# Expert outputs of a four-layer model: ScalarE copies both banks, and products with a stacked identity add and turn them

## The reference

```python
h = tok(ids, adj, rel)                                 # embeddings and a neighbour sum
h = h + attn0(norm(h)); h = h + experts16(norm(h))     # 16 experts, 2 chosen, relu, then a norm
h = h + attn1(norm(h)); h = h + experts4(norm(h))      # 4 experts, routed by attention over a graph, gelu
h = h + attn2(norm(h)); h = h + experts8(norm(h))      # 8 experts, 2 chosen, gelu
h = h + attn3(norm(h)); h = h + experts8_gated(norm(h))# 8 experts, silu(x w1) * (x w3), then w2
# every expert part:
out = sum over e of gate[:, e] * (act(x @ w1[e] + b1[e]) @ w2[e] + b2[e])
```

## Time and profile before

| | |
|---|---|
| runs of the kernel before | 947.99, 953.34, 950.22 us; median 950.22 |
| the profiled execution | 948.82 us |
| its span, first to last instruction | 947.0 us |
| mean granted TensorE clock | 0.933 of full speed |
| TensorE busy | 828.5 us |
| VectorE busy | 642.7 us |
| ScalarE busy | 372.0 us |
| POOL busy | 231.4 us |

### The profile page before, as it was taken

One profiled execution on the slowest core, in us unless ns is written; L12 is line 12 of the kernel. 1 busy time (PEld: TensorE's weight loads), 2 busy tenths in 40 slices (PEclk: granted clock), 3 DMA queues, 4 the chain that ended last, 5 costly groups with the idle time before them and its releaser, 6 DMA issues. The chain is left out here.

```text
span 947.0 us, 18228 instructions
## 1 busy us (share of the span) xinstructions
PE 828.5 (87%) x7272; PEld 455.8 (48%) x7272; DVE 642.7 (68%) x1722; ACT 372.0 (39%) x644; POOL 231.4 (24%) x292
## 2 busy tenths in 40 slices
PE   0896879979997887998888879999999998987997
PEld 0466757755533335773366533333333444444543
DVE  3979558878885548997754776556566457557665
ACT  0222444344653343223542523545454333244433
POOL 1900003314535113440150041113132414110000
PEclk9898989988999999998975987999999999797999
DMA  9500030000000001000000000000000000000000
GB/s 295 136 1 2 1 94 2 2 2 2 1 1 2 0 2 48 1 2 1 1 1 1 2 1 1 1 1 2 1 1 2 1 2 1 2 1 1 7 7 12
DMA packets 11360, 15.16 MB, mean 16 GB/s; under 512 B 8262, under 2 KB 9318, under 8 KB 10278
## 3 DMA queue, kind: packets, MB, share of 16 engines
q1 hardware_dynamic: 9856, 12.89, 4.4%
q10 hardware_dynamic: 1418, 1.09, 0.5%
HBM read 13.45 MB, written 0.52 MB: 15 GB/s over the span
## 5 line engine op out<-in xcount | busy, mean ns | idle before, releaser
L996 DVE TENSOR_REDUCE mx<-PS 128x2 f32<-128x1024 f32 (+3 forms) x96 | 102.5, 1088 | 69.5 <-PE PS L772 57.8
L937 ACT ACTIVATE arena<-PS 128x1024 f32<-128x1024 f32 (+3 forms) x96 | 85.8, 917 | 126.4 <-PE PS L813 113.4
L804 PE MATMUL PS<-arena 32*128 32x512 f32 (+3 forms) x384 | 88.7, 609 | 6.7 <-ACT arena L923 2.7
L829 PE MATMUL PS<-arena 128*64 128x512 f32 (+3 forms) x384 | 93.5, 571 | 0.4 <-DVE arena L1055 0.4
L772 PE MATMUL PS<-arena 32*128 32x512 f32 (+3 forms) x384 | 89.7, 635 | 4.4 <-DVE arena L979 3.8
L1537 ACT ACTIVATE arena<-PS,f_b_sb 128x512 f32<-128x512 f32 x96 | 61.2, 684 | 42.0 <-PE PS L1468 38.9
L1563 DVE TENSOR_TENSOR arena<-arena,PS 128x512 f32<-128x512 f32 x96 | 61.6, 683 | 16.0 <-PE PS L1479 15.9
L1468 PE MATMUL PS<-XT,late 64*64 64x512 f32 x384 | 62.5, 621 | 2.7 <-issue 1.3
L1499 PE MATMUL PS<-arena,late 64*64 64x512 f32 x384 | 57.3, 595 | 0.9 <-DVE arena L1563 0.9
L1100 POOL TENSOR_TENSOR H<-H,arena 128x256 f32<-128x256 f32 x32 | 23.5, 735 | 120.1 <-DVE arena L1030 117.7
L804 PEld LDWEIGHTS PS<-arena 32*128 32x128 f32 x384 | 27.3, 189 | 51.3 <-issue 32.8
(11 more groups left out here) (481 smaller groups left out, 1761.0 us busy)
## 6 DMA issues: line engine op xcount, KB each, us to landing
arena<-in_rel SPq DMA_DIRECT2D x4, 1024.0 KB, 12.0
late<-in_edges SPq DMA_DIRECT2D x2, 1024.0 KB, 11.5
arena<-in_adj SPq DMA_DIRECT2D x1, 1024.0 KB, 6.9
late<-in_w_f_w SPq DMA_DIRECT2D x2, 512.0 KB, 3.9
Cc<-in_consts SPq DMA_DIRECT2D x1, 916.0 KB
arena<-in_ids ACTq DMA_DIRECT2D x1, 800.0 KB
late<-in_w_f_w SPq DMA_DIRECT2D x2, 340.0 KB, 3.7
late<-in_w_f_w SPq DMA_DIRECT2D x4, 128.0 KB, 2.8
```

What stands on the lines that cost most here:

```text
L804: ins = nc.tensor.matmul(PS[:, a + j, queries(g, c)], KT[h, g % 3, c * P:(c + 1) * P], QT[h, g % 3, queries(g, c)], start=not less_first, ...
L829: ins = nc.tensor.matmul(PS[half(j), 6 + p, queries(g, c)], XO[:, batch(g) * TB + c, :], PT[:, s % 2, p, j, queries(g, c)], start=c == 0, ...
L937: nc.scalar.activation(PT[:, s % 2, p, :, queries(g, c)], PS[:, a:a + 2, queries(g, c)], ACT.Exp, scale=of(g).scale).then_inc(exp_done.sem, 1)
L996: v.reduce_max(mx[:, g % 2, c, 2 * p:2 * p + 2], PS[:, a:a + 2, keys(g, c)], axis=AX.X).then_inc(max_done.sem, 1)
```

## The change

ScalarE now copies both banks, into `OT` and a new `OT2`, and counts `out_copied` up by two a batch. VectorE's sum is gone, with `out_summed`. The turn is no longer four transposes but eight f32 products with `C["twin"]` as the moving operand: for each of four chunks of 128 tokens one product has the chunk of `OT` as weights and one the chunk of `OT2`, both accumulated in the same 64 columns of PSUM. A product with `twin` turns the chunk and adds its two halves of partitions; the accumulation adds the two banks. So what comes out is the batch's output itself, 256 columns instead of 512, and VectorE adds it to the residual in one addition instead of two. `half_added` is gone. TensorE's wait before the next batch's first `down` and before the turn is now for both copies.

```diff
@@ shared
     OT = part(3584, [2, S])
+    OT2 = part(4608, [2, S])
-    out_summed = Signal(ctx, nc, "out_summed")
-    half_added = Signal(ctx, nc, "half_added")
@@ experts, TensorE
                         if b >= 1:
-                            eng.wait_ge(out_copied.sem, c0 + b)
+                            eng.wait_ge(out_copied.sem, c0 + 2 * b)
                         if b >= 2:
                             eng.wait_ge(out_added.sem, a0 + b - 1)
...
                 def turn(b):
-                    eng.wait_ge(out_summed.sem, s0 + b + 1)
+                    eng.wait_ge(out_copied.sem, c0 + 2 * b + 2)
                     for t in range(TB):
-                        ins = nc.tensor.transpose(PS[:, out_banks(b)[1], t * P:(t + 1) * P], OT[:, b % 2, t * P:(t + 1) * P], ident)
+                        for part_sums in (OT, OT2):
+                            ins = nc.tensor.matmul(PS[:, out_banks(b)[1], t * D:(t + 1) * D], part_sums[:, b % 2, t * P:(t + 1) * P], C["twin"], start=part_sums is OT, stop=part_sums is OT2, skip_group_check=True)
                     ins.then_inc(turned_done.sem, 1)
@@ experts, ScalarE
                         nc.scalar.copy(OT[:, b % 2, :], PS[:, out_banks(b)[0], :]).then_inc(out_copied.sem, 1)
+                        nc.scalar.copy(OT2[:, b % 2, :], PS[:, out_banks(b)[1], :]).then_inc(out_copied.sem, 1)
@@ experts, VectorE
-                        turned = PS[:, out_banks(b)[1], :].rearrange("p (t m d) -> p t m d", m=2, d=D)
+                        turned = PS[:, out_banks(b)[1], 0:TB * D].rearrange("p (t d) -> p t d", d=D)
                         eng.wait_ge(turned_done.sem, t0 + b + 1)
-                        v.tensor_tensor(dst[:, y, :], turned[:, :, 0], base[:, y, :], ALU.add).then_inc(half_added.sem, 1)
-                        eng.wait_ge(half_added.sem, f0 + b + 1)
-                        v.tensor_tensor(dst[:, y, :], turned[:, :, 1], dst[:, y, :], ALU.add).then_inc(out_added.sem, 1)
+                        v.tensor_tensor(dst[:, y, :], turned, base[:, y, :], ALU.add).then_inc(out_added.sem, 1)
...
-                    if ends(k - LAG):
-                        b = tiles[2 * (k - LAG)][0]
-                        eng.wait_ge(out_copied.sem, c0 + b + 1)
-                        v.tensor_tensor(OT[:, b % 2, :], PS[:, out_banks(b)[1], :], OT[:, b % 2, :], ALU.add).then_inc(out_summed.sem, 1)
```

More of the change, by code:

```diff
@@ L1433, in experts @@
         u0, g0, d0, t0 = up_done.count, gates_done.count, down_done.count, turned_done.count
-        h0, k0, c0, s0, f0, a0 = hidden_done.count, gated_done.count, out_copied.count, out_summed.count, half_added.count, out_added.count
+        h0, k0, c0, a0 = hidden_done.count, gated_done.count, out_copied.count, out_added.count
         RU, RG = 3, 2
@@ L1585, in _ @@
                 eng.wait_ge(out_added.sem, a0 + B)
-        for signal, n in ((up_done, U), (gates_done, U), (down_done, U), (turned_done, B), (hidden_done, U), (gated_done, U), (out_copied, B), (out_summed, B),
-                          (half_added, B), (out_added, B)):
+        for signal, n in ((up_done, U), (gates_done, U), (down_done, U), (turned_done, B), (hidden_done, U), (gated_done, U), (out_copied, 2 * B),
+                          (out_added, B)):
             signal.count += n
@@ L1608, in experts_by_gated_inputs @@
         u0, l0, g0, d0, t0 = up_done.count, linear_done.count, gates_done.count, down_done.count, turned_done.count
-        h0, x0, k0, c0, s0, f0, a0 = hidden_done.count, inputs_gated.count, gated_done.count, out_copied.count, out_summed.count, half_added.count, out_added.count
+        h0, x0, k0, c0, a0 = hidden_done.count, inputs_gated.count, gated_done.count, out_copied.count, out_added.count
         def pair(r):
@@ L1749, in _ @@
                             entered["last_gates_out"]()
[L1750 to L1753, removed]
                     if 2 <= j <= U + 1 and steps[j - 2][1] == SPB - 1:
@@ L1756, in _ @@
                         y = slice(b * TB, (b + 1) * TB)
-                        turned = PS[:, out_banks(b)[1], :].rearrange("p (t m d) -> p t m d", m=2, d=D)
+                        turned = PS[:, out_banks(b)[1], 0:TB * D].rearrange("p (t d) -> p t d", d=D)
                         eng.wait_ge(turned_done.sem, t0 + b + 1)
-                        nc.vector.tensor_tensor(dst[:, y, :], turned[:, :, 0], base[:, y, :], ALU.add).then_inc(half_added.sem, 1)
-                        eng.wait_ge(half_added.sem, f0 + b + 1)
-                        nc.vector.tensor_tensor(dst[:, y, :], turned[:, :, 1], dst[:, y, :], ALU.add).then_inc(out_added.sem, 1)
+                        nc.vector.tensor_tensor(dst[:, y, :], turned, base[:, y, :], ALU.add).then_inc(out_added.sem, 1)
                 eng.wait_ge(out_added.sem, a0 + B)
         for signal, k in ((up_done, U), (linear_done, U), (gates_done, 4 * B), (down_done, U), (turned_done, B), (hidden_done, 2 * U), (inputs_gated, 4 * B),
-                          (gated_done, 2 * U), (out_copied, B), (out_summed, B), (half_added, B), (out_added, B)):
+                          (gated_done, 2 * U), (out_copied, 2 * B), (out_added, B)):
             signal.count += k
```

## The result

The changed kernel takes 971.61 us, the median of four runs (970.15 to 975.41); the kernel before, beside it, 949.11 (four runs). The ratio is 1.0229, with a 95% interval of 1.0179 to 1.028. The forecast was 958.5 in a range of 952 to 967: slower, as said, but by 22.5 us instead of 8.3. The first rival's number, 971, is where it came out.

The account below looks back on a forecast made before the run. TensorE was taken to bound the expert stages. Stage terms of 2.7, 3.15, 0.8 and 1.65 us summed to 8.3, added to the 950.22 us median for 958.5 us, range 952 to 967.

Parts of the forecast that it names:

- The first rival: Turns on TensorE: each of 16 records costs 0.113 us, 20.7 us more in all, so 971 us; chance 0.12.
- TensorE bounds these stages: Four expert stages: TensorE sets the pace and VectorE follows, so work taken from VectorE is worth little.
- 16 records in place of four: Each batch's turn on TensorE: eight f32 products of two records each stand where four transposes took one each.
- The price of a record: Turn on TensorE: records 0.059 us apart, so each turn takes 0.55 us more.
- Loads don't hide: Rival on the turns: weight loads aren't hidden, 0.113 us a record, 1.37 us more a turn, 971 us; chance 0.12.
- The holds: TensorE's wait for both copies ahead of the next batch: about 0.58, 0.45 and, in two stages, 0.47 us added.
- the last stage's zero: Hold in the last stage: two rounds of products lie between copy and wait, so nothing is added.
- The stage ends: Bare chain ending a stage: turn 0.14 us sooner, 0.55 longer, half addition's 0.46 gone; sum -0.05, nothing.
- 0.14 sooner: End of a stage: the turn starts at 466.95 instead of 467.09 us, after two copies of 0.586 each.
- The third stage: End of the third stage: VectorE is on the path, its relief absorbs part of the delay, leaving 0.8 us.
- Slack takes it: Rival: TensorE's waits elsewhere shrink, absorbing the holds and half of the turns; 3.3 us more, 953.5 us; chance 0.21.
- relief wins: Rival: VectorE's 18.2 us really delays TensorE at the first three stages' gate multiplications; 6.2 us gained, 944 us; chance 0.07.

Follow-up runs that it names:

- the one with 128 columns: The changed kernel with the 128x128 identity as moving operand, 128 columns streamed per product, and two half additions on VectorE: 968.16 us, 1.0178 to the kernel before.

## Why the prediction was wrong, step by step

- *TensorE bounds these stages.* Right, and the reason that the sign was right. VectorE's relief of 17 us turned into waiting.
- *16 records in place of four.* Right: 192 for 12 batches.
- ***The price of a record* is the step that failed.** "I take 0.059, because rows and columns agree with the new form." It was 0.112. The two starts 0.06 us apart weren't a rate, and the trace of before had the answer in the loads, not in the products. The loads of those two products, and of the transposes:

```profile
139.69 0.19 PEld L1238 LDWEIGHTS PS<-arena 128*128 128x128 f32 x1
...
139.80 0.19 PEld L1238 LDWEIGHTS PS<-arena 128*128 128x128 f32 x1
...
L1506 PEld LDWEIGHTS PS<-Cc,arena x48: 138/140/143, 245.5 to 556.6; 128*128 128x128 f32 x48
```

The two loads start at 139.69 and 139.80, 0.11 apart. The first one's product could start only at 139.80, behind a longer product ahead of it (128 columns); the second one's load began at that moment, and its product followed 0.06 later. So a late product made the starts of the products bunch, while the loads kept their distance. That a product's record starts 0.06 behind its load's doesn't mean, then, that the load is done in 0.06: the last record is 0.28 us long, the one ahead of it, of as many columns, 0.22. This fits a product that waits for its weights inside its own record, and is read from the records alone. The turn of before had about the same step, too: its transposes, with weights as wide, were taken in the prediction as "three steps of 0.11". (They stream 128 columns; whether their load or their product sets that step no run here shows.) The change put 16 records of such a step where 4 stood, and that they stream half the columns each shortens nothing. The miss of 19.3 - 8.3 = 11.0 us is then the turn's: nine turns in mid-stage at 1.34 instead of 0.55 are 7.1, three bare ends at 0.64 that were put at nothing 1.9, the third stage 2.6. That makes 11.6; the holds, shorter than forecast, take some 0.4 off it.
- *Loads don't hide*, the rival, had the right price, from L2112, and half of the mechanism: the loads don't hide, but the products hide behind them. That its 971 us were met to within 1 us is partly luck: it put 20.7 us into the stages, where 19.3 were measured, and the rest lies outside them. With the full height and 128 columns, load and product do overlap, so the rule that was weighed (overlap only when the row group differs) doesn't describe these runs.
- *The holds.* 4.0 us were forecast in three stages (1.03, 1.50, 1.50); taking them away gave 0.83, 1.20 and 1.32. Right in the main, a little too high; so is the last stage's zero, where what that run lost is its slow turn's.
- *The stage ends.* "0.14 sooner" was 0.25, since the second copy starts 0.48 us behind the first (480.69 and 481.17), not 0.586. With the turn at 1.34 more, the end came out 0.64 longer, not 0.05 shorter.
- *The third stage* absorbed some, as forecast: 3.41 where its turns and holds alone come to 1.3 + 4 x 1.34 = 6.7. (The sum there is 0.68 us long, not 0.60; that changes little.)
- *Slack takes it* and *relief wins*: no stage became shorter, or grew by less than forecast, so the stages show neither.

## What to carry to other kernels

Price a product by its load as well as by its columns: a chain of small f32 products with fresh 128-column weights runs at the loads' pace, and streaming fewer columns than 128 gains nothing. With more columns the product may be what shows. In L1238's chain, with loads of 128, the second product of 192 columns is followed after 0.16 us (139.41 to 139.58), one of 128 after 0.11 (139.58 to 139.69); that is one pair each, and wasn't tested. Read a rate from the starts of both rows, loads and products, over a long chain; a single pair behind a longer instruction shows a queue draining. Where one engine sets the pace, work taken off another and put on it is paid in full, as in three of the four stages here, and a wait placed ahead of a queue should name only the write that it protects. Before sums of stages are compared, begin them where the edit begins, and look at the granted clock inside them.

## What was not expected of the hardware

- f32 loads of 64 columns into the two column halves of the array go side by side: 32 records in the time of 16 (1.08 us either way).
- The record of a transpose's f32 load of 128 columns lasts 140 ns, an f32 product's of the same width 192, and one of 64 columns 138; the steps are 0.109, 0.112 and 0.058 us. So the length of a load's record alone doesn't tell the step.
- Some 10 us at half the granted clock sat behind the first stage in both traces of the changed kernel, and neither in the kernel before nor in the one with 128 columns, though the latter's turns are as long: 3.3 us. Behind the third stage the kernel before had such a stretch and the changed one had none.
- The way to the second stage's first copy, the same work in every kernel here, takes 6.3 to 8.0 us, at a mean granted clock of 0.91 to 0.68.
